# A 3x3 layer in five pairs of taps instead of six, with a second, row-shifted copy of its input

## The chip, the cores and the metric

The kernel runs on one NeuronCore of a Trainium2 chip. The metric is the device time in microseconds (us) of one launch, lower is better; the median of several runs is quoted. Engines are named as in the profile: PE (TensorE matmuls), PEld (its weight loads), DVE (VectorE), ACT (ScalarE), POOL (GpSimd), SP (SyncE, which issues all of this kernel's DMAs; SPq is its queue).

## What is computed

A batch of 16 images, 256 channels, 32 x 32 pixels, in float32, goes through two stages.

```python
# stage 0: attention block
xn   = group_norm(x, 32 groups) * gn_w + gn_b
qkv  = einsum('oc,bchw->bohw', qkv_w, xn) + qkv_b        # q, k, v: 4 heads of 64
attn = softmax(einsum('bhdm,bhdn->bhmn', q, k) / 8)      # 1024 x 1024 per head
out  = einsum('bhmn,bhdn->bhdm', attn, v)
x    = x + einsum('oc,bchw->bohw', proj_w, out) + proj_b
# stage 1: three conv layers whose weights are mixed per image from 8 experts
rw  = sigmoid(x.mean(h, w) @ router_w.T + router_b)      # 8 gates per image
out = relu(bn1(conv1x1(x,   sum_e rw[e] * w1[e])))       # 256 -> 64
out = relu(bn2(conv3x3(out, sum_e rw[e] * w2[e])))       # 64 -> 64, padding 1
out = bn3(conv1x1(out,      sum_e rw[e] * w3[e]))        # 64 -> 256
x   = relu(out + x)
```

## The kernel before

Everything of an image lies in SBUF. The attention of image i is cut into 32 steps (STEPS): two pairs of heads, two halves of the queries, eight blocks of 128 keys. For each step PE makes the scores of two heads into one of two PSUM buffers `S` (L706 and L709, four matmuls), ACT takes the exponential into `prob` (L795), POOL adds it up over the eight key blocks (L556), and PE multiplies it with V into the bank `PV` (L722); the last is done for four steps at a time, a "turn". A further pair of matmuls per step (L688, "max fill") computes scores for a later block into the bank pair `MS`, and DVE reduces these to row maxima (L922). A fill may only write a half of `MS` when DVE has reduced what was there.

All other work is cut into jobs that stand between the steps at fixed places. PE, ACT and DVE walk through the same list in the same order. The table `PLACES` gives, for each step n, the jobs that PE does behind that step's scores and fill; `HALVES` gives those behind a turn's L722 matmuls. `WORK` places their DVE part, `ACT_WORK` and `POOL_WORK` place further work of ACT and POOL, `LOADS` the loads on SP. An entry is (kind, image offset, index): offset -1 is the image whose attention ended, for which the conv layers are done, +1 is the next one, whose q, k and v are prepared.

The jobs that matter here:

- `qk` (L582, six matmuls of 512 columns in three-term float32r form): q or k of a head pair and a half. ACT copies the bank with bias to Q or K in two halves (L810), DVE makes the remainder in two halves (L959), and only then is the bank `SB` free.
- `v` (L582, six matmuls of 256 columns): one key block of v. ACT copies it out in two pieces (L816, L817).
- `row` (L631): a row of maxima; DVE copies it out (L934).
- `proj` (L626), `gna` and `gnb` (L592, L595: statistics of the group norm), `z` (L616: sums of the softmax, into one half of `MS`).
- `conv1` (L649): ACT writes the result with batch norm and relu into `hpad`, four instructions at L840. `hpad` is a padded image of 34 x 34 pixels: partitions 0 to 63 hold the 64 channels, partitions 64 to 127 the same shifted by one pixel.
- `conv2a` and `conv2` (L662), directly behind each other in turn 5: the 3x3 layer. Since the upper partitions hold the neighbour to the right, one matmul with 128 rows computes two taps of a row: (dy, 0) with (dy, 1). The taps (dy, 2) stand alone, their upper weights are zero. So TAPS = 6 pairs, each for two halves of the image (output partitions 0 to 63 and 64 to 127 of the bank): 12 matmuls per image.
- `mix`: the weights of the three layers, mixed from 8 experts. An expert is 128 x MIX numbers, MIX = 128 + TAPS * 64 + 256 = 768. ACT multiplies each with its gate (`product`, L856), POOL adds them (L513), SP loads them (L387). conv1 waits for the last addition.

All of these jobs share one bank, `SB`. Each PE job waits until the job before it has been read out (`held`). PE therefore waits wherever two jobs with a slow reader follow each other closely.

An image's iteration runs steps 0 to 31. The first and the last image have programs of their own; the last image's conv layers come at the end with nothing beside them.

Of the kernel before, what the change touches and what calls it, by code (L numbers as in the profile page):

```python
# [89 lines left out]
WORK = {1: [("qk", 0, 6)], 2: [("proj", -1, 0)], 3: [("row", 0, 1), ("stats", 1, 0), ("stats", 1, 1), ("recip", -1, 3), ("gna", 1, 0)],  # L90
        4: [("proj", -1, 1), ("gnb", 1, 0)], 7: [("qk", 0, 7)], 8: [("proj", -1, 2)], 9: [("proj", -1, 3)],
        10: [("router", -1, 0), ("gates", -1, 0), ("row", 0, 2)], 14: [("qk", 1, 0), ("qk", 1, 1)], 16: [("qk", 1, 2)],
        18: [("row", 0, 3), ("recip", 0, 0)], 22: [("recip", 0, 1), ("qk", 1, 3)], 26: [("recip", 0, 2), ("row", 1, 0)],
        27: [("conv3", -1, 0), ("conv3", -1, 1)], 29: [("qk", 1, 4)], 31: [("qk", 1, 5), ("conv3", -1, 2), ("conv3", -1, 3)]}
# [1049 lines left out]
```

## Time and profile before

| | |
|---|---|
| runs | 2052.08, 2053.33, 2059.14 us; median 2053.33 us |
| the profiled execution | 2058.66 us, of which the traced span 2056.9 us |
| PE busy | 1891.7 us, 92% of the span |
| POOL, ACT, DVE busy | 71%, 53%, 51% |

The span is the time from the first to the last traced instruction; some 1.8 us lie outside of it. An image takes 124.2 to 125.9 us from one 3x3 layer to the next. Idle times in brackets at the end of a row are those of the row's engine just before it, with what released it. fp32 matmuls leave two records for one instruction, so the 12 matmuls of L662 show as x24.

### The profile page before, as it was taken

How to read it: one execution, taken by the hardware profiler on the slowest of the kernel's cores; microseconds unless marked ns; L12 is line 12 of the kernel's file. 1: busy time of each engine (PE TensorE's matmuls, PEld its weight loads, DVE VectorE, ACT ScalarE, POOL GpSimd, SP SyncE). 2: the span in 40 equal slices, each digit the busy share in tenths (PEclk: the TensorE clock that was granted, in tenths of full speed). 3: DMA queues.
4: the chain of work that ended last, by engine and by line, in shares of the span. 5: the costliest groups of instructions: out<-in, count | busy, mean ns of one | idle time of the engine just before them, and what ended most of it. 6: DMA issues, size and time to landing. Idle time of an engine off the chain costs nothing.

```text
span 2056.9 us, 28956 instructions
## 1 busy us (share of the span) xinstructions
PE 1891.7 (92%) x8388; PEld 1073.6 (52%) x8388; DVE 1042.4 (51%) x1812; ACT 1089.9 (53%) x1498; POOL 1453.5 (71%) x829
## 2 busy tenths in 40 slices
...
GB/s 90 46 49 62 108 83 73 82 62 92 86 88 76 59 86 82 97 77 74 80 61 107 77 77 82 62 92 87 87 82 56 83 82 97 77 68 70 57 103 82
DMA packets 94113, 161.58 MB, mean 79 GB/s; under 512 B 25600, under 2 KB 26368, under 8 KB 94080
## 3 DMA queue, kind: packets, MB, share of 16 engines
...
q8 instruction: 17, 0.28, 0.1%
...
## 4 chain that ended last, share of the span: by engine, by line
PE 78%; issue 7%; DVE 6%; ACT 5%; POOL 2%; DMA 1%; DVEq 0%; ACTq 0%; SPq 0%; POOLq 0%
PE PV L722 22%; PE SB L582 13%; PE MS L688 10%; PE S L706 9%; PE S L709 8%; PE SB L626 5%; PE SB L662 4%; DVE K L959 2%; POOL psum_p L556 2%; PE SB L671 1%; PE SB L649 1%; PE MS L616 1%; DVE mx L922 1%; ACT Q L810 1%; ACT hpad L840 1%
## 5 line engine op out<-in xcount | busy, mean ns | idle before, releaser
L556 POOL TENSOR_TENSOR psum_p<-psum_p,prob 128x1024 f32<-128x1024 f32 x384 | 914.2, 2381 | 197.5 <-ACT prob L795 178.6
L922 DVE TENSOR_REDUCE mx<-MS 128x1 f32<-128x512 f32 x998 | 641.8, 685 | 597.3 <-PE MS L688 589.3
L795 ACT ACTIVATE prob<-S 128x1024 f32<-128x1024 f32 x512 | 519.5, 1023 | 301.3 <-PE S L709 297.8
L722 PE MATMUL PV<-prob,V 128*64 128x512 f32 x2048 | 475.6, 607 | 0.0
L706 PE MATMUL S<-Q,K 128*128 128x512 f32 x1024 | 445.0, 435 | 13.0 <-ACT prob L795 10.0
L709 PE MATMUL S<-Q,K 128*128 128x512 f32 x1024 | 402.1, 393 | 0.0
L688 PE MATMUL MS<-K,Q 128*128 128x512 f32 x998 | 336.8, 405 | 34.1 <-ACT zrow L828 11.9
L722 PEld LDWEIGHTS PV<-prob,V 128*64 128x64 f32 x2048 | 137.4, 138 | 259.9 <-issue 229.7
L706 PEld LDWEIGHTS S<-Q,K 128*128 128x128 f32 x1024 | 192.5, 188 | 152.4 <-issue 86.8
L688 PEld LDWEIGHTS MS<-K,Q 128*128 128x128 f32 x998 | 184.8, 187 | 123.4 <-DVE mx L922 52.2
L513 POOL TENSOR_TENSOR mix<-mix,ex 128x768 f32<-128x768 f32 x90 | 165.0, 1833 | 74.7 <-ACT ex L856 72.8
L709 PEld LDWEIGHTS S<-Q,K 128*128 128x128 f32 x1024 | 192.9, 188 | 45.2 <-issue 14.3
L556 POOL TENSOR_TENSOR psum_p<-prob 128x1024 f32<-128x1024 f32 x64 | 152.1, 2376 | 78.5 <-ACT prob L795 78.5
L518 POOL TENSOR_TENSOR o<-o,rz 128x512 f32<-128x512 f32 x63 | 80.8, 1282 | 83.4 <-DMA rz<-z_dram 83.4
L626 PE MATMUL SB<-o,wp 128*128 128x512 f32 x244 | 117.7, 604 | 22.3 <-DVE Q L959 16.5
L856 ACT ACTIVATE ex<-ex,rw 128x768 f32<-128x768 f32 x120 | 110.6, 933 | 23.9 <-DMA ex<-in_experts_dram 23.2
L582 PE MATMUL SB<-x_hi,w_hi 128*128 128x512 f32 x246 | 102.0, 414 | 22.7 <-DVE K L959 18.8
L810 ACT ACTIVATE Q<-SB,vec 64x512 fp32r<-64x512 f32 x124 | 85.0, 685 | 68.0 <-PE SB L582 66.5
L959 DVE SCALAR_TENSOR_TENSOR Q<-SB,vec,Q 64x512 fp32r<-64x512 f32 x124 | 92.9, 749 | 52.8 <-ACT Q L810 51.9
L959 DVE SCALAR_TENSOR_TENSOR K<-SB,vec,K 64x512 fp32r<-64x512 f32 x122 | 91.5, 750 | 55.0 <-ACT K L810 53.1
L810 ACT ACTIVATE K<-SB,vec 64x512 fp32r<-64x512 f32 x122 | 83.5, 684 | 67.7 <-PE SB L582 38.3
L582 PE MATMUL SB<-x_lo,w_hi 128*128 128x512 f32 x246 | 97.2, 395 | 0.0
...
## 6 DMA issues: line engine op xcount, KB each, us to landing
ex<-in_experts_dram SPq DMA_DIRECT2D x122, 384.0 KB, 3.5
...
K<-K SPq DMA_DIRECT2D x128, 128.0 KB, 2.3
Q<-Q SPq DMA_DIRECT2D x128, 128.0 KB, 2.2
...
rz<-z_dram SPq DMA_DIRECT2D x126, 128.0 KB, 2.9
V<-v_next SPq DMA_DIRECT2D x16, 512.0 KB, 2.9
```

The source lines that it names most:

```text
L513: nc.gpsimd.tensor_tensor(mix[:, :], others, ex[:, e % 2, :], ALU.add).then_inc(mix_chain, 1)
L556: nc.gpsimd.tensor_tensor(acc, first_in, prob[:, s % PBUF, :, :], ALU.add).then_inc(add_done, 1)
L582: last = nc.tensor.matmul(dst, wl(w, c), xl(m, c), start=(k == 0), stop=(k == 3 * CC - 1))
L626: last = nc.tensor.matmul(bank, wp[:, c, oc * P:oc * P + P], o[:, c, px(hf)], start=(c == 0), stop=(c == CC - 1))
L688: nc.tensor.matmul(MS[:, nh, :], Q1[:, h, q0:q0 + P], K1[:, h, px(nh)], start=True, stop=True).then_inc(max_filled, 1)
L706: nc.tensor.matmul(S[:, s % 2, a, :], K1[:, h, kt * P:kt * P + P], Q1[:, h, px(hf)], start=True, stop=False)
L709: last = nc.tensor.matmul(S[:, s % 2, a, :], K2[:, h, kt * P:kt * P + P], Q2[:, h, px(hf)], start=False, stop=True)
L722: last = nc.tensor.matmul(PV[own(a), :], V[:, b // NH, kt, a * D:a * D + D], prob[:, s % PBUF, a, :], start=(kt == 0), stop=(kt == KT - 1))
L795: nc.scalar.activation(prob[:, s % PBUF, :, :], S[:, s % 2, :, :], ACT.Exp, scale=D ** -0.5).then_inc(exp_done, 1)
L810: nc.scalar.activation(dst[own(a), 2 * p + a, px(hf)], bank[own(a), :], ACT.Identity, bias=vec[own(a), col:col + 1]).then_inc(qk_hi, 1)
L922: nc.vector.reduce_max(mx[:, b % 2, nh, m:m + 1], MS[:, nh, :], AX.X).then_inc(max_read, 1)
L959: last = nc.vector.scalar_tensor_tensor(out=dst, in0=bank[own(a), :], scalar=vec[own(a), col:col + 1], in1=hi[own(a), h, px(hf)].bitcast(F ...
```

## The change

TAPS becomes 5. Taps (0,2) and (1,2), which stood alone, form one pair: a new tile `hrow` (128 x 1156) holds the 64 channels unshifted in its lower partitions and shifted by one row in its upper ones, so that a matmul at (0, 2) computes (0,2) and (1,2) together. Tap (2,2) stays alone and is computed from `hpad`. `hrow` is filled from the lower half of `hpad` by two DMAs on SP (64 x 1156 and 64 x 1122 floats, 289 and 280.5 KB) in step 21, behind a wait for conv1's last ACT write. `conv2a` now does four pairs from `hpad`; `conv2`, behind a new wait for both DMAs, does the fifth from `hrow`. MIX becomes 704, so that each expert's load, product and addition are 8% smaller. The host packs the weights in the new order.

The tables move: on PE, `qk` 6 goes from step 1 to 0, `qk` 7 from 5 to 6, `v` 0 of the next image from 19 to 18. On DVE, these follow (`qk` 6 to step 0), the statistics are split over steps 2 and 3, the reciprocals go from 3 to 4, 18 to 16, 26 to 27, `qk` 3 from 22 to 23, `row` 0 from 26 to 27, `qk` 5 from 31 to 30. On ACT, `normal` 0 goes from 6 to 5, product 2 from 13 to 14, product 5 from 16 to 17. On POOL, `deviations` goes from 4 to 5, mix 5 from 16 to 17, mix 6 and 7 from 18 to 19, `norm` 3, 0, 1 from 7, 19, 24 to 6, 23, 29. Of the loads, V goes from 2 to 7, two of x from 21 to 20 and 25.

```diff
-TAPS = 6
+TAPS = 5
...
-          12: [("qk", 1, 0)], 15: [("qk", 1, 1)], 16: [("qk", 1, 2)], 19: [("v", 1, 0), ("row", 0, 3), ("v", 1, 1), ("v", 1, 2)],
+          12: [("qk", 1, 0)], 15: [("qk", 1, 1)], 16: [("qk", 1, 2)], 18: [("v", 1, 0)], 19: [("row", 0, 3), ("v", 1, 1), ("v", 1, 2)],
...
-LOADS = {2: [("v1", 0, 0)], 17: [("xin", 2, 0)], 21: [("xin", 2, 1), ("xin", 2, 2)], 29: [("xin", 2, 3)]}
+LOADS = {7: [("v1", 0, 0)], 17: [("xin", 2, 0)], 20: [("xin", 2, 1)], 21: [("h", -1, 0)], 25: [("xin", 2, 2)], 29: [("xin", 2, 3)]}
...
+        hrow = sb("hrow", [P, PAD])
...
+            def copy_h(i):
+
+                sp.wait_ge(read["conv1"], i + 1)
+                sp.dma_start(hrow[own(0), :], hpad[own(0), 0:PAD]).then_inc(hrow_loaded, 16)
+                sp.dma_start(hrow[own(1), 0:PAD - PW], hpad[own(0), PW:PAD]).then_inc(hrow_loaded, 16)
...
+                        if kind == "h" and not first:
+                            copy_h(i + di)
...
+            copy_h(B - 1)
             for f in range(4):
                 store(B - 1, f)
...
-                    for tap in (range(3) if kind == "conv2a" else range(3, 6)):
-                        dy, dx = tap % 3, 2 * (tap // 3)
+                    if kind == "conv2":
+                        pe.wait_ge(hrow_loaded, 32 * i + 32)
+                    for tap in (range(4) if kind == "conv2a" else (4,)):
+                        dy, dx = ((0, 0), (1, 0), (2, 0), (2, 2), (0, 2))[tap]
+                        source = hpad if kind == "conv2a" else hrow
                         for hf in range(NH):
                             at = (dy + hf * rows_hf) * PW + dx
-                            src = hpad[:, at:at + rows_hf * PW].rearrange("p (r w) -> p r w", w=PW)[:, :, 0:W]
+                            src = source[:, at:at + rows_hf * PW].rearrange("p (r w) -> p r w", w=PW)[:, :, 0:W]
...
-    low = np.concatenate([w2[0], w2[2]], axis=2)
-    high = np.concatenate([w2[1], np.zeros_like(w2[1])], axis=2)
+    low = np.concatenate([w2[0], w2[2][:, :, 2:3], w2[2][:, :, 0:1]], axis=2)
+    high = np.concatenate([w2[1], np.zeros_like(w2[1][:, :, 0:1]), w2[2][:, :, 1:2]], axis=2)
```

How this moves PE's instructions in the loop over the images, at three places. Line numbers of the changed kernel are larger by 11 to 14: L593 is L582, L642 is L631, L676 is L662, L702 is L688, L720 and L723 are L706 and L709, L936 and L973 are DVE's L922 and L959. The rows with ISA or REGISTER_ALU are waits and register arithmetic.

First, PE around step 19, before: the end of `v` 0, the row of maxima, the start of `v` 1.

```order
L688 MATMUL MS<-K1,Q1 128x512 x2
L582 MATMUL SB<-w_hi,x_hi 128x256
L582 MATMUL SB<-w_hi,x_lo 128x256
L582 MATMUL SB<-w_lo,x_hi 128x256
L582 MATMUL SB<-w_hi,x_hi 128x256
L582 MATMUL SB<-w_hi,x_lo 128x256
L582 MATMUL SB<-w_lo,x_hi 128x256
L630 REGISTER_ALU
L631 MATMUL SB<-negeye,mx1 8x128
L582 MATMUL SB<-w_hi,x_hi 128x256
```

And after:

```order
L593 MATMUL SB<-w_hi,x_lo 128x256
L593 MATMUL SB<-w_lo,x_hi 128x256
L720 MATMUL S<-Q1,K1 128x512
L723 MATMUL S<-Q2,K2 128x512
L720 MATMUL S<-Q1,K1 128x512
L723 MATMUL S<-Q2,K2 128x512
L698 ISA
L701 ISA
L702 MATMUL MS<-K1,Q1 128x512 x2
L641 REGISTER_ALU
L642 MATMUL SB<-negeye,mx1 8x128
L593 MATMUL SB<-w_hi,x_hi 128x256
```

Step 19's scores and fill now stand between `v` 0 and the row; the row and `v` 1, and `v` 1 and `v` 2, still follow each other directly.

Second, DVE at the start of the iteration, steps 0 and 1, before:

```order
L922 TENSOR_REDUCE mx<-MS 128x1
L921 ISA
L922 TENSOR_REDUCE mx<-MS 128x1
L921 REGISTER_ALU
L922 TENSOR_REDUCE mx<-MS 128x1
L957 ISA
L959 SCALAR_TENSOR_TENSOR Q<-SB,vec,Q 64x512
L957 REGISTER_ALU
L959 SCALAR_TENSOR_TENSOR Q<-SB,vec,Q 64x512
L921 ISA
```

And after:

```order
L936 TENSOR_REDUCE mx<-MS 128x1
L971 ISA
L973 SCALAR_TENSOR_TENSOR Q<-SB,vec,Q 64x512
L971 REGISTER_ALU
L973 SCALAR_TENSOR_TENSOR Q<-SB,vec,Q 64x512
L935 ISA
L936 TENSOR_REDUCE mx<-MS 128x1
L935 REGISTER_ALU
L936 TENSOR_REDUCE mx<-MS 128x1
```

The two halves of `qk` 6 moved ahead of the reductions of step 1's fill.

Third, PE at the 3x3 layer in turn 5, before:

```order
L722 MATMUL PV<-prob,V 64x512 x8
L662 MATMUL SB<-hpad,mix 64x512 x12
L609 REGISTER_ALU
L286 ISA
L616 MATMUL MS<-psum_p,ones 32x256 x4
L706 MATMUL S<-Q1,K1 128x512
```

And after:

```order
L736 MATMUL PV<-prob,V 64x512 x8
L676 MATMUL SB<-hpad,mix 64x512 x8
L669 ISA
L676 MATMUL SB<-hrow,mix 64x512 x2
L620 REGISTER_ALU
L288 ISA
L627 MATMUL MS<-psum_p,ones 32x256 x4
L720 MATMUL S<-Q1,K1 128x512
```

Two matmuls are gone, and a wait (L669) stands ahead of the last two.

## Rows read from the trace of the kernel before

**Rows 1.** The page's part 1: busy us, share of span, instructions.

```profile
PE 1891.7 (92%) x8388; PEld 1073.6 (52%) x8388; DVE 1042.4 (51%) x1812; ACT 1089.9 (53%) x1498; POOL 1453.5 (71%) x829
```

**Rows 2.** Who PE waited for in one image, 753 to 878 us: total, times, longest.

```profile
PE SB L582 <- DVE K L959: 1.3, 2, 0.9
PE SB L626 <- DVE Q L959: 1.1, 1, 1.1
```

**Rows 3.** One line's instructions, L662: first and last start, in three images.

```profile
L662 PE MATMUL SB<-hpad,mix x24: 592/592/592, 753.1 to 757.9; 128*64 128x512 f32 x24
L662 PE MATMUL SB<-hpad,mix x24: 592/592/593, 877.5 to 882.2; 128*64 128x512 f32 x24
L662 PE MATMUL SB<-hpad,mix x24: 592/592/593, 1003.3 to 1008.0; 128*64 128x512 f32 x24
```

**Rows 4.** Timeline of turn 5: start us, us, engine, line, operation.

```profile
877.46 5.32 PE L662 MATMUL SB<-hpad,mix 128*64 128x512 f32 x24
...
882.71 0.64 PE L616 MATMUL MS<-psum_p,ones 128*32 128x256 f32 x8
```

**Rows 5.** Timeline: conv1 and its write of hpad.

```profile
863.36 1.94 PE L649 MATMUL SB<-x,mix 128*64 128x512 f32 x8
...
865.34 3.15 ACT L840 ACTIVATE hpad<-SB,bn_c,bn_s 64x512 f32<-64x512 f32 x4 [1.46 <-PE SB L649]
```

**Rows 6.** The page's part 6: DMA issues, KB each, us to landing.

```profile
ex<-in_experts_dram SPq DMA_DIRECT2D x122, 384.0 KB, 3.5
...
K<-K SPq DMA_DIRECT2D x128, 128.0 KB, 2.3
...
V<-v_next SPq DMA_DIRECT2D x16, 512.0 KB, 2.9
```

**Rows 7.** Timeline of PE, steps 18 and 19.

```profile
852.06 1.09 PE L688 MATMUL MS<-K,Q 128*128 128x512 f32 x2 [0.76 <-DVE mx L922]
...
854.97 0.28 PE L582 MATMUL SB<-w_lo,x_hi 128*128 128x256 f32 x1
855.95 0.38 PE L631 MATMUL SB<-negeye,mx 128*8 128x128 f32 x2 [0.69 <-ACT v_next L817]
856.79 0.39 PE L582 MATMUL SB<-w_hi,x_hi 128*128 128x256 f32 x1 [0.46 <-DVE mrow L934]
...
858.30 0.39 PE L582 MATMUL SB<-w_hi,x_hi 128*128 128x256 f32 x1 [0.53 <-ACT v_next L817]
```

**Rows 8.** Timeline of PE and DVE, steps 0 to 2.

```profile
790.20 0.72 PE L688 MATMUL MS<-K,Q 128*128 128x512 f32 x2 [0.91 <-ACT zrow L828]
...
794.81 1.51 DVE L959 SCALAR_TENSOR_TENSOR Q<-SB,vec,Q 64x512 fp32r<-64x512 f32 x2 [1.41 <-ACT Q L810]
...
796.45 1.98 PE L626 MATMUL SB<-o,wp 128*128 128x512 f32 x4 [1.12 <-DVE Q L959]
```

**Rows 9.** Timeline of PE in step 5.

```profile
809.55 0.50 PE L582 MATMUL SB<-x_hi,w_hi 128*128 128x512 f32 x1 [0.26 <-DVE gvar_of L949]
```

**Rows 10.** Timeline of POOL, steps 17 to 19.

```profile
858.12 1.84 POOL L513 TENSOR_TENSOR mix<-mix,ex 128x768 f32<-128x768 f32 x1
860.73 1.82 POOL L513 TENSOR_TENSOR mix<-mix,ex 128x768 f32<-128x768 f32 x1 [0.77 <-ACT ex L856]
```

**Rows 11.** Busy us by stretch: PE, PEld, DVE, ACT, POOL, granted clock, DMA share, GB/s.

```profile
358.00:361.00 3.00, 2.90 (x10) 1.89 (x12) 0.00 (x0) 1.26 (x4) 1.75 (x1) 0.50 0.28 84
...
858.00:861.00 3.00, 2.70 (x16) 1.42 (x18) 0.17 (x1) 1.52 (x5) 2.23 (x3) 1.00 0.30 62
983.00:986.00 3.00, 3.00 (x12) 1.54 (x13) 0.00 (x0) 1.27 (x3) 1.56 (x2) 0.51 0.46 112
...
1607.50:1610.50 3.00, 3.00 (x10) 1.58 (x11) 0.00 (x0) 1.27 (x3) 1.54 (x2) 0.50 0.38 112
1734.00:1737.00 3.00, 3.00 (x10) 0.93 (x11) 0.00 (x0) 1.27 (x3) 1.92 (x2) 0.52 0.62 167
```

More of the change, by code:

```diff
@@ L72 @@
 TURNS = STEPS // BATCH
-PLACES = {1: [("qk", 0, 6)], 2: [("proj", -1, 0)], 3: [("row", 0, 1)], 4: [("gna", 1, 0), ("proj", -1, 1)],
-          5: [("gnb", 1, 0), ("qk", 0, 7)], 8: [("proj", -1, 2)], 9: [("proj", -1, 3)], 10: [("router", -1, 0)], 11: [("row", 0, 2)],
[1 row of a table removed]
+PLACES = {0: [("qk", 0, 6)], 2: [("proj", -1, 0)], 3: [("row", 0, 1)], 4: [("gna", 1, 0), ("proj", -1, 1)], 5: [("gnb", 1, 0)],
+          6: [("qk", 0, 7)], 8: [("proj", -1, 2)], 9: [("proj", -1, 3)], 10: [("router", -1, 0)], 11: [("row", 0, 2)],
[1 row of a table added]
           21: [("v", 1, 3)], 22: [("qk", 1, 3)], 24: [("v", 1, 4)], 25: [("v", 1, 5)], 26: [("v", 1, 6)], 27: [("row", 1, 0)],
@@ L87 @@
 FIRST_PAIRS = 8 + AHEAD
[L90 to L94, printed above, removed]
@@ L108 @@
-LOADS = {2: [("v1", 0, 0)], 17: [("xin", 2, 0)], 21: [("xin", 2, 1), ("xin", 2, 2)], 29: [("xin", 2, 3)]}
+WORK = {0: [("qk", 0, 6)], 2: [("proj", -1, 0), ("stats", 1, 0)], 3: [("row", 0, 1), ("stats", 1, 1), ("gna", 1, 0)],
+        4: [("proj", -1, 1), ("recip", -1, 3), ("gnb", 1, 0)], 7: [("qk", 0, 7)], 8: [("proj", -1, 2)], 9: [("proj", -1, 3)],
+        10: [("router", -1, 0), ("gates", -1, 0), ("row", 0, 2)], 14: [("qk", 1, 0), ("qk", 1, 1)], 16: [("recip", 0, 0), ("qk", 1, 2)],
+        18: [("row", 0, 3)], 22: [("recip", 0, 1)], 23: [("qk", 1, 3)],
+        27: [("recip", 0, 2), ("row", 1, 0), ("conv3", -1, 0), ("conv3", -1, 1)], 29: [("qk", 1, 4)], 30: [("qk", 1, 5)],
+        31: [("conv3", -1, 2), ("conv3", -1, 3)]}
```

13 lines of the change are left out of this document (7 added, 6 removed).

## The prediction

> **What bounds the kernel now.** I read the page's busy shares first. PE is busy 92% of the span, POOL 71%, ACT and DVE about half [rows 1]. So outside the start and the end PE sets the time, and another engine counts only where PE waits for it. Next I read who PE waited for in one steady image [rows 2]. Eleven kinds of wait, 0.3 to 1.3 us each, make 7.2 us of about 124; two of them stand there. Most are waits for the shared bank `SB`: a job was computed, ACT and DVE had not read it out, and the next job was already due. Third comes the length of an image. The 3x3 layer starts at 753.1, 877.5 and 1003.3 us: 124.4 us for one image, 125.8 for the next [rows 3]. The busy table with the granted clock tells them apart: at 983 to 986 us the clock is 0.51, which is 1.2 GHz instead of 2.4 [rows 11]. There are six such falls between 350 and 1740 us, four of which stand there. Each follows the same place of the image, the waits of step 19, which in a plain image end at 858.3 us [rows 7] with the clock at 1.00 behind them [rows 11]. 877.5 - 858.3 is 19.2 us ahead of the next 3x3 layer; 1003.3 - 19.2 = 984, inside the low stretch of that image. An image with such a fall takes 1.4 to 1.6 us more.
>
> **The base of the sum.** The profiled execution took 2058.66 us, the traced span is 2056.9. The median is 2053.33, so this execution was 5.3 us slower than the median. I sum against 2058.66 and take off less where the falls of the clock stay.
>
> **Part 1, the sixth pair of taps goes.** The 12 matmuls take from 877.46 to 882.71 us, when `z` starts [rows 4]: 5.25 us, 0.875 us for each tap's two halves. The two halves use different columns of the array and overlap, so the pair, not the matmul (0.59 us each in rows 3), is the unit. One pair fewer per image is 16 x 0.875 = 14.0 us, all of it on PE. Behind the layer PE goes on with `z` and scores, and no row there shows it waiting, so nothing takes the place of the time saved in steady images.
>
> **Part 2, the new wait for hrow.** No row shows such a copy. Its bounds: a 128 KB copy inside SBUF lands in 2.3 us, a 512 KB one in 2.9, a 384 KB load from memory in 3.5 [rows 6]. The copies have 289 and 280 KB. I take 2.9 us each, nearest in size and kind, and half a us for the second issue: 3.4 us; range 2.3 to 5. `hpad` is complete at 865.34 + 3.15 = 868.5 us [rows 5]. SP reaches the copy in step 21, behind loads whose conditions hold by then, so they land at about 872. The fifth pair is due at 877.46 + 4 x 0.875 = 881.0 [rows 4]: 9 us of cover, price nothing. What is queued on SP behind its wait for conv1 are `qk` 3's two copies and a reciprocal's transfers of step 22, which aren't ready before that either. At the very end the cover is only the four pairs: 3.5 us at full clock, against 3.4, so 0 to 1.5 us once. I take 0.
>
> **Part 3, smaller experts.** An addition of 1.83 us [rows 10] falls to about 704/768 of it, 1.69. That is POOL's and ACT's time; PE sees it only at conv1, which waits for the last addition. That ends at 860.73 + 1.82 = 862.55, and conv1 starts at 863.36 [rows 5, 10]. In the new table mix 6 and 7 stand behind the sums of steps 18 and 19, where before step 19's sum (2.36 to 2.4 us, like the others) came after them; so the last mix could end later. Mix 5 is done at about 854.0 (ACT's product of 852.3 and 1.69 us), then two sums to 858.8, mix 6 to 860.4, mix 7 to 862.1. PE comes to conv1 0.8 us earlier (part 4), at 862.6. So I price it at nothing, with 0 to 0.6 us an image for the range.
>
> **Part 4, the waits that the tables move.** In step 19 `v` 0, the row, `v` 1 and `v` 2 follow each other, with waits of 0.69, 0.46 and 0.53 us [rows 7]. With `v` 0 in step 18, scores and a fill (1.4 us) lie between it and the row, and ACT's copy is done. The start of the row after the start of the last `v` 0 matmul, 855.95 - 854.97 = 0.98 us, shrinks to what back-to-back matmuls take, 0.12 to 0.2: 0.8 us gone. The other two stay. `qk` 6 in step 0 instead of 1: the 1.12 us wait of `proj` goes [rows 8], but DVE now does the two halves of `qk` 6 (1.51 us) ahead of step 1's two reductions (1.3 us). `qk` 6 comes 1.65 us earlier, DVE ends it at 796.3 - 1.65 = 794.7 and the reductions at 796.0, and step 2's fill needs these. `proj`, which waits behind this fill, starts at 796.2 instead of 796.45. So a new wait eats most of the old: 0.2 us gone. `qk` 7 in step 6: its wait of 0.26 us [rows 9] goes, but step 6's fill comes sooner after step 5's reductions; 0.1 us gone. The 0.91 us for `zrow` [rows 8], 0.76 ahead of step 18's fill [rows 7] and 1.3 us for `K` in two places [rows 2] stay, since nothing moved that they hang on. The other moves change POOL, DVE and SP at places where PE doesn't wait. Together 1.1 us an image; 15 images have these places: 16.5 us. Bounds: below, 0 if each wait moves on to the next reader; above, the whole of the three waits with the restart, 0.8 + 1.1 + 0.3 = 2.2 us, 33 us.
>
> **Part 5, the clock.** The falls begin right behind step 19's waits, where PE stood 1.7 us out of some 3.5 [rows 7]; 0.7 us of that goes. The places that keep more than 1 us of waiting close together, steps 0 to 2 with 0.91 and 1.12 us [rows 8], have no fall in any image. I therefore expect the six falls to go: 6 x 1.55 = 9.3 us. The least is 0. The page "TensorE: Matmul & The Clock Gate" of the Trainium skill, in "A second HAM failure mode: psum-queue depth-cycling", tells that frequent short idles between groups of matmuls make the clock swing between its levels; the trace agrees, since no wait at these places is over 0.7 us.
>
> **The sum.** 2058.66 - 14.0 - 0 - 0 - 16.5 - 9.3 = 2018.9, say 2019 us.
>
> **The rivals.**
>
> *The falls of the clock stay.* Then their six places are set by something else than these 0.7 us: 2019 + 9.3 = 2028 us. For it speaks that only 6 of 15 equal images have one, so the waits alone don't decide. Against it, that all six stand at one place. The table in "Why this matters for your kernels" on the same page of the Trainium skill names only idle gaps longer than any wait of this image as what drops the clock mid-kernel; by it removing 0.7 us would change nothing and the time would be this rival's, while the six rows at the lower clock behind short waits speak against that rule.
>
> *The moves bring nothing.* Each wait on `SB` is handed to the next reader, as in step 2, and only the matmuls and the clock count: 2058.66 - 14.0 - 9.3 = 2035 us. For it: PE's margin over DVE's reductions is thin everywhere, fills wait 0.76 us already. Against: step 19's row waits for two ACT copies of 0.28 us, which are long done one step later.
>
> *hrow comes late, and the kernel gets slower.* The mechanism is SP's single in-order queue. If the copy stood behind a load whose condition comes late, the fifth pair waits in each image, PE's queue behind it (`z`, the scores of step 24, thus ACT's exponentials) stands too. It eats part 1 from 0.9 us of waiting on, and with parts 4 and 5 it makes the kernel slower by 0.3% only from (39.8 + 6) / 16 = 2.9 us an image on, i.e. if the copies land after 881.0 + 2.9 = 883.9, 15 us after `hpad` is there. At that price it is 2060 or more. The rows of SBUF copies (2.3 to 2.9 us) are far from it. In the milder form, that the change doesn't save its matmuls because the fifth pair waits 0.9 us, the time is 2019 + 14 = 2033.
>
> *More goes than I count.* If DVE's order at step 0 costs nothing and all three waits go, 2058.66 - 14.0 - 33 - 9.3 = 2002; half of this is 2010.
>
> **How the numbers follow.** Forecast 0.5 (2013 to 2024); falls of the clock stay in whole or part 0.2 (2024 to 2030); moves bring little, or hrow waits a little 0.17 (2030 to 2045); more goes 0.09 (2002 to 2013); slower 0.04. The range that leaves 2 in 10 out at most is 2010 to 2037. About 0.3% of the time, 6 us, is what a measurement can tell from no change. Faster by more than that 0.94, within it 0.03, slower 0.03. Nearly all cases lie on one side because PE loses 14 us of work on the path, and only an hrow 12 us late turns it.
>
> **What would show it.** Right: L662's successor shows x20 records per image and 4.4 us; an image takes 122.3 to 122.5 us; no wait of PE for hrow's DMAs; the row in step 19 has no wait in front, while a fill waits about 0.8 to 1.2 us for DVE in step 2; the clock reads 1.00 in the middle images. Wrong: an idle time of PE at the fifth pair, one at conv1 released by POOL's mix (part 3), stretches at 0.5 of the clock behind step 19, or images of 123.4 us or more.

## The result, and the profile after

| | kernel before | changed kernel |
|---|---|---|
| time, median (range) of 4 runs each, side by side | 2053.66 us (2052.08 to 2059.14) | 2021.76 us (2020.85 to 2023.01) |
| profiled execution / its span | 2058.66 / 2056.9 us | 2022.01 / 2020.2 us |
| one plain image, between starts of the 3x3 layer (mean) | 124.29 us | 122.33 us |
| one image with a fall of the clock | 125.7 to 125.9 us | none left |
| mean granted clock of TensorE, 260 to 1880 us | 0.99, six falls | 1.00, no fall |

The changed kernel takes 0.984 of the time before, interval 0.982 to 0.986. The medians lie 31.9 us apart and the two profiled executions 36.65, because the profiled execution of the kernel before was 5 us slower than its median.

The wait list of PE for one steady image of the changed kernel answers to [rows 2] (columns: engine, what it accesses, line; what it waited for; us in total, times, longest):

```profile
PE MS L702 <- DVE mx L936: 1.6, 2, 0.9
PE SB L593 <- DVE K L973: 1.3, 2, 0.9
PE MS L702 <- ACT zrow L842: 0.9, 1, 0.9
PE SB L593 <- ACT v_next L831: 0.5, 1, 0.5
PE SB L593 <- DVE mrow L948: 0.5, 1, 0.5
...
PE S L720 <- ACT prob L809: 0.4, 1, 0.4
```

Eight kinds are left of eleven, 6.0 us of 7.2. The wait for `Q` (1.1 us) has gone, and a second wait of a fill for `mx` has come. The four records of the 3x3 layer, by their source line, in two images that follow each other, answer to [rows 3]:

```profile
L676 PE MATMUL SB<-hpad,mix x16: 592/592/592, 738.7 to 741.7; 128*64 128x512 f32 x16
L676 PE MATMUL SB<-hrow,mix x4: 592/592/592, 742.1 to 742.6; 128*64 128x512 f32 x4
...
L676 PE MATMUL SB<-hpad,mix x16: 592/592/592, 861.0 to 864.0; 128*64 128x512 f32 x16
L676 PE MATMUL SB<-hrow,mix x4: 592/592/592, 864.5 to 864.9; 128*64 128x512 f32 x4
```

The reader is to see three things: 20 records instead of 24; no gap between the pairs from `hpad` and the one from `hrow` (the matmuls of both halves start together, and a new start comes every 0.43 us throughout), hence no wait for the copy; and 861.0 - 738.7 = 122.3 us for the image.

Steps 18 and 19 in the changed kernel's timeline of PE answer to [rows 7] (start, duration, engine, line, operation, tiles, idle before and its releaser):

```profile
836.40 1.09 PE L702 MATMUL MS<-K,Q 128*128 128x512 f32 x2 [0.76 <-DVE mx L936]
...
838.95 0.61 PE L702 MATMUL MS<-K,Q 128*128 128x512 f32 x2
839.50 0.39 PE L642 MATMUL SB<-negeye,mx 128*8 128x128 f32 x2
...
840.35 0.39 PE L593 MATMUL SB<-w_hi,x_hi 128*128 128x256 f32 x1 [0.46 <-DVE mrow L948]
...
841.85 0.39 PE L593 MATMUL SB<-w_hi,x_hi 128*128 128x256 f32 x1 [0.53 <-ACT v_next L831]
```

The row of maxima (L642) stands straight behind the fill; its wait of 0.69 us is gone, the other two are the same. Steps 0 to 2, first PE and then DVE, answer to [rows 8]:

```profile
774.88 0.73 PE L702 MATMUL MS<-K,Q 128*128 128x512 f32 x2 [0.91 <-ACT zrow L842]
...
780.15 1.10 PE L702 MATMUL MS<-K,Q 128*128 128x512 f32 x2 [0.86 <-DVE mx L936]
781.08 1.88 PE L637 MATMUL SB<-o,wp 128*128 128x512 f32 x4
```

```profile
777.85 1.52 DVE L973 SCALAR_TENSOR_TENSOR Q<-SB,vec,Q 64x512 fp32r<-64x512 f32 x2 [1.15 <-ACT Q L824]
779.40 2.58 DVE L936 TENSOR_REDUCE mx<-MS 128x1 f32<-128x512 f32 x4
```

`proj` (L637) no longer waits, but the fill ahead of it does, for reductions that now start behind the 1.52 us for `Q`.

The clock and the engines by stretches (start:end, length, busy time and instructions of PE, PEld, DVE, ACT, POOL, then granted clock, DMA share, GB/s), in the changed kernel over the middle and right behind step 19, answer to [rows 11]:

```profile
260.00:1880.00 1620.00, 1534.34 (x6887) 874.58 (x6885) 847.79 (x1483) 895.83 (x1246) 1188.48 (x672) 1.00 0.30 84
841.00:844.00 3.00, 2.47 (x15) 1.37 (x15) 0.53 (x1) 1.57 (x5) 3.00 (x2) 1.00 0.40 155
```

**Where the 36.65 us between the two profiled executions went.** The first start of the 3x3 layer moved from 253.0 to 249.4 us: 3.6 (1.7 of it a wait for the DMA into `Q` that the first image no longer has). The 13 images behind it took 1625.0 us (253.0 to 1878.0) and now 1590.2 (249.4 to 1839.6): 34.8, which is 13 x 1.96 = 25.5 for a plain image, and 9.3 for the six falls. The stretch from the last of these starts to the end gave back 1.7 us: 178.9 before, 180.6 after. 3.6 + 34.8 - 1.7 = 36.7.

### The profile page after: what moved, and what is told of

Its sections match the earlier page's. It is cut to its first block, busy times and chain, and to the rows that moved or that the text cites. A ratio compares the mean times of both kernels' runs of the same rounds, so it can differ in the third digit from the quotient of the medians.

```text
span 2020.2 us, 28886 instructions
## 1 busy us (share of the span) xinstructions
PE 1868.8 (93%) x8324; PEld 1063.3 (53%) x8324; DVE 1040.8 (52%) x1812; ACT 1079.9 (53%) x1498; POOL 1437.7 (71%) x829
## 4 chain that ended last, share of the span: by engine, by line
PE 75%; issue 8%; DVE 8%; ACT 5%; POOL 3%; DMA 0%; DVEq 0%; ACTq 0%; SPq 0%; POOLq 0%
PE PV L736 21%; PE SB L593 13%; PE MS L702 9%; PE S L720 9%; PE S L723 7%; PE SB L637 5%; PE SB L676 4%; DVE mx L936 3%; DVE K L973 2%; POOL psum_p L567 2%; PE SB L660 1%; PE SB L685 1%; PE MS L627 1%; ACT hpad L854 1%; ACT Q L824 1%
## 5 line engine op out<-in xcount | busy, mean ns | idle before, releaser
L936 DVE TENSOR_REDUCE mx<-MS 128x1 f32<-128x512 f32 x998 | 642.4, 686 | 544.9 <-PE MS L702 539.7
L736 PE MATMUL PV<-prob,V 128*64 128x512 f32 x2048 | 467.7, 598 | 0.0
L720 PE MATMUL S<-Q,K 128*128 128x512 f32 x1024 | 446.7, 436 | 12.8 <-ACT prob L809 9.8
L723 PE MATMUL S<-Q,K 128*128 128x512 f32 x1024 | 402.4, 393 | 0.0
L702 PE MATMUL MS<-K,Q 128*128 128x512 f32 x998 | 340.3, 409 | 48.7 <-DVE mx L936 24.8
L720 PEld LDWEIGHTS S<-Q,K 128*128 128x128 f32 x1024 | 192.6, 188 | 151.2 <-issue 98.2
L702 PEld LDWEIGHTS MS<-K,Q 128*128 128x128 f32 x998 | 185.2, 188 | 143.9 <-DVE mx L936 76.7
L723 PEld LDWEIGHTS S<-Q,K 128*128 128x128 f32 x1024 | 193.2, 189 | 43.8 <-issue 14.3
L524 POOL TENSOR_TENSOR mix<-mix,ex 128x704 f32<-128x704 f32 x90 | 152.6, 1696 | 46.1 <-ACT ex L870 43.1
L973 DVE SCALAR_TENSOR_TENSOR K<-SB,vec,K 64x512 fp32r<-64x512 f32 x122 | 91.4, 750 | 71.7 <-ACT K L824 70.3
L637 PE MATMUL SB<-o,wp 128*128 128x512 f32 x244 | 117.7, 605 | 5.8 <-DVE gsum L956 5.1
L870 ACT ACTIVATE ex<-ex,rw 128x704 f32<-128x704 f32 x120 | 102.7, 879 | 36.7 <-DMA ex<-in_experts_dram 32.7
L973 DVE SCALAR_TENSOR_TENSOR Q<-SB,vec,Q 64x512 fp32r<-64x512 f32 x124 | 92.8, 749 | 52.7 <-ACT Q L824 51.8
L593 PE MATMUL SB<-x_hi,w_hi 128*128 128x512 f32 x246 | 100.3, 408 | 18.9 <-DVE K L973 18.9
L593 PE MATMUL SB<-x_lo,w_hi 128*128 128x512 f32 x246 | 97.2, 395 | 0.0
```

Source lines behind the costliest of these rows:

```text
L524: nc.gpsimd.tensor_tensor(mix[:, :], others, ex[:, e % 2, :], ALU.add).then_inc(mix_chain, 1)
L593: last = nc.tensor.matmul(dst, wl(w, c), xl(m, c), start=(k == 0), stop=(k == 3 * CC - 1))
L637: last = nc.tensor.matmul(bank, wp[:, c, oc * P:oc * P + P], o[:, c, px(hf)], start=(c == 0), stop=(c == CC - 1))
L702: nc.tensor.matmul(MS[:, nh, :], Q1[:, h, q0:q0 + P], K1[:, h, px(nh)], start=True, stop=True).then_inc(max_filled, 1)
L720: nc.tensor.matmul(S[:, s % 2, a, :], K1[:, h, kt * P:kt * P + P], Q1[:, h, px(hf)], start=True, stop=False)
L723: last = nc.tensor.matmul(S[:, s % 2, a, :], K2[:, h, kt * P:kt * P + P], Q2[:, h, px(hf)], start=False, stop=True)
```

## Experiments

All edits are against the changed kernel unless "before" is named. Each batch was timed beside the kernel before, on another chip each time. That kernel's median was 2060.1 us beside the first four runs, 2058.8 beside the next four and 2058.3 beside the last three, against 2053.7 beside the changed kernel, which was not timed again. In ratios, the changed kernel stands at 0.984; a ratio that differs from this by 0.002 or 0.003 can come from the kernel before alone, and so can a few us between medians. What an edit does to a steady image is therefore read from the traces. "Plain image" is the mean of those without a fall; "falls" counts the images with one behind the first 3x3 layer.

| experiment | median, us | ratio to before (interval) | plain image, us | falls |
|---|---|---|---|---|
| pairs_only | 2042.76 | 0.991 (0.990 to 0.993) | 123.49 | 4 |
| moves_only | 2041.35 | 0.991 (0.989 to 0.993) | 123.60 | 0 |
| v0_only | 2038.43 | 0.990 (0.988 to 0.991) | 123.51 | 0 |
| v0_back | 2034.51 | 0.988 (0.986 to 0.989) | 123.10 | 1 |
| late_copy | 2051.68 | 0.997 (0.996 to 0.999) | 123.9 to 124.4 | 0 |
| no_copy | 2023.03 | 0.982 (0.980 to 0.983) | 122.31 | 0 |
| qk6_back | 2027.04 | 0.984 (0.983 to 0.986) | 122.49 | 0 |
| mix_back | 2020.01 | 0.981 (0.980 to 0.982) | 122.35 | 0 |
| v_spread | 2042.72 | 0.993 (0.990 to 0.995) | 123.62 | 4 |
| v_spread_qk5 | 2047.78 | 0.995 (0.993 to 0.996) | 123.80 | 5 |
| all_three | 2008.68 | 0.976 (0.973 to 0.978) | 121.56 | 0 |

### The two halves of the change apart

**pairs_only** keeps the five pairs, the copies and the smaller experts, and takes the tables of the kernel before.

PLACES, WORK, ACT_WORK and POOL_WORK are those of the kernel before word for word, and LOADS with the copy added:

```diff
-LOADS = {7: [("v1", 0, 0)], 17: [("xin", 2, 0)], 20: [("xin", 2, 1)], 21: [("h", -1, 0)], 25: [("xin", 2, 2)], 29: [("xin", 2, 3)]}
+LOADS = {2: [("v1", 0, 0)], 17: [("xin", 2, 0)], 21: [("xin", 2, 1), ("xin", 2, 2), ("h", -1, 0)], 29: [("xin", 2, 3)]}
```

> The changed kernel with all tables of places of the kernel before (the copy to hrow is added in step 21). Theory: a pair is 0.875 us of PE's path, 16 x 0.875 = 14.0 us; the waits of step 19 (0.69, 0.46, 0.53) stay, and with them the falls of the clock to 1.2 GHz behind step 19. So 2053.7 - 14 = 2040 us, an image of 123.4 us without a fall and 125.0 with one. Rival A (matmuls alone change the clock): no falls, 2058.7 - 14 - 9.3 = 2035. Rival B (the fifth pair waits for hrow or something else takes the place of the pair): 2045 to 2054.

Measured 2042.76 us (2040.22 to 2045.64). A plain image takes 123.49 us, 0.8 less than before: the price of one pair of taps. The copy and the smaller experts are in it too, but PE's eleven waits add up to 7.2 us as before. The falls did not go: four images take 125.1 us. Two of them, in stretches behind step 19:

```profile
731.00:734.00 3.00, 2.91 (x10) 1.57 (x12) 0.00 (x0) 1.25 (x4) 1.57 (x2) 0.58 0.18 65
1103.00:1106.00 3.00, 2.87 (x10) 1.56 (x12) 0.00 (x0) 1.29 (x4) 1.61 (x2) 0.59 0.26 84
```

They stand 372 us apart, three images; every third image has one. Fewer matmuls alone don't keep the clock up. The stretch behind the 14th start of the 3x3 layer, with three such layers in it, is 175.8 us long against 178.9 before.

**moves_only** is the kernel before with the tables of the changed one, and so with six pairs, 768 columns of each expert and no copy.

All five tables are replaced; of them the loads:

```diff
-LOADS = {2: [("v1", 0, 0)], 17: [("xin", 2, 0)], 21: [("xin", 2, 1), ("xin", 2, 2)], 29: [("xin", 2, 3)]}
+LOADS = {7: [("v1", 0, 0)], 17: [("xin", 2, 0)], 20: [("xin", 2, 1)], 25: [("xin", 2, 2)], 29: [("xin", 2, 3)]}
```

> The kernel before with the tables of places of the changed one (six pairs, experts of 768 columns, no hrow). Theory: waits of 1.1 us an image go in 15 images and the falls of the clock go: 2058.7 - 16.5 - 9.3 = 2033; since experts stay large and mix 6 and 7 stand later, conv1 may now wait up to 0.6 us an image for the last addition, 2033 to 2042. Rival (the moves are worth nothing, waits are handed on): 2049 to 2054.

Measured 2041.35 us (2040.32 to 2042.54), 123.6 us an image and no fall. The tables alone are worth 0.7 us an image. The changed kernel is 1.27 us shorter per image, and the pair is 0.8 to 0.86 of that. Of the remaining 0.4, 0.33 is the last line of this kernel's wait list for an image, which neither the kernel before nor the changed one has:

```profile
PE SB L649 <- POOL mix L513: 0.3, 1, 0.3
```

With experts of 768 columns and the later places, POOL's last addition ends behind the point at which conv1 is due. With 704 columns it ends just ahead of it. In the changed kernel's timeline the last addition ends at 846.76 us and conv1 starts at 846.92, a margin of 0.16 us. No run changes the size of the experts alone, so that it is the size that makes this difference is argued from the lengths of the additions (1.68 us against 1.83), not shown by itself.

```profile
845.08 1.68 POOL L524 TENSOR_TENSOR mix<-mix,ex 128x704 f32<-128x704 f32 x1
...
846.92 1.94 PE L660 MATMUL SB<-x,mix 128*64 128x512 f32 x8
```

### Which move removes the falls

**v0_only** is the kernel before with one entry moved.

```diff
-          12: [("qk", 1, 0)], 15: [("qk", 1, 1)], 16: [("qk", 1, 2)], 19: [("v", 1, 0), ("row", 0, 3), ("v", 1, 1), ("v", 1, 2)],
+          12: [("qk", 1, 0)], 15: [("qk", 1, 1)], 16: [("qk", 1, 2)], 18: [("v", 1, 0)], 19: [("row", 0, 3), ("v", 1, 1), ("v", 1, 2)],
```

> The kernel before with one place changed: v 0 of the next image in step 18 instead of 19, on PE and ACT. Theory: 0.8 us an image go in 15 images (12 us), and with 0.7 us less of waiting in step 19 the clock never falls in the middle images (9.3 us): 2058.7 - 12 - 9.3 = 2037, granted clock 1.00 in the stretches behind step 19. Rival (the falls have another cause): six or so falls stay, 2058.7 - 12 = 2047 for an execution with six, an image of 123.4 us where the clock holds and 125.0 where it falls.

Measured 2038.43 us (2037.88 to 2039.23): 123.51 us an image, 0.78 less than before, and no fall. The middle of this kernel reads

```profile
260.00:1880.00 1620.00, 1531.32 (x6882) 871.50 (x6881) 839.65 (x1470) 895.16 (x1237) 1193.62 (x668) 1.00 0.28 80
```

with the clock at 1.00. An image is as long as in pairs_only to 0.02 us, and that kernel, with the wait ahead of the row still in it, has four falls. So it isn't the length of the image that keeps the falls away here, it is the wait that went. One entry of one table gives 1.0 of the changed kernel's 1.6 per cent.

**v0_back** is the changed kernel with that entry put back, the reverse of the diff above.

> The changed kernel with v 0 put back to step 19, the rest unchanged. Theory: the wait of 0.69 us ahead of the row returns, 12 us, and the falls of the clock behind step 19 return, some 3 to 6 of them at 1.5 us: 2021.8 + 12 + 4.5 to 9.3 = 2038 to 2043. Rival (the falls don't hang on this wait): 2034, clock 1.00 throughout the middle.

Measured 2034.51 us (2033.0 to 2035.33): 123.1 us an image, so 0.77 lost, as expected. But three to six falls were expected back, and only one came, in one image of 124.7 us:

```profile
1216.00:1219.00 3.00, 2.82 (x10) 1.53 (x12) 0.00 (x0) 1.34 (x4) 2.67 (x3) 0.61 0.01 2
```

Each image of v0_back has the same 1.7 us of waits close together as each of pairs_only and of the kernel before. They have one, four and six falls. Of the kernels in which one of these waits is gone, those of v_spread and v_spread_qk5 below have falls, at a wait of 2.2 us elsewhere, and all others have none. So the waits let a fall happen, but they don't decide in which image it comes.

### What the copy costs

**late_copy** issues it one step later.

```diff
-LOADS = {7: [("v1", 0, 0)], 17: [("xin", 2, 0)], 20: [("xin", 2, 1)], 21: [("h", -1, 0)], 25: [("xin", 2, 2)], 29: [("xin", 2, 3)]}
+LOADS = {7: [("v1", 0, 0)], 17: [("xin", 2, 0)], 20: [("xin", 2, 1)], 22: [("h", -1, 0)], 25: [("xin", 2, 2)], 29: [("xin", 2, 3)]}
```

> The changed kernel with the copy to hrow in step 22 instead of 21, behind qk 3's copies and a reciprocal's transfers on SP's in-order queue (which issue last at 861.2 us in the changed kernel's trace, while the copy issues at 852.1). Theory: the cover of 9 us goes, the copy issues at about 861.3 and 861.9 and lands 3.2 and 4.0 us later, 865.9; the fifth pair is due at 864.5, so it waits 1.4 us an image, 16 x 1.4 = 22 us: 2044. Rival (such a wait costs nothing, since the scores behind it have slack): 2022 to 2026.

Measured 2051.68 us (2047.55 to 2054.89). The expectation was 2044. SP comes to the copy only at 871.31 us, when the 3x3 layer has started (871.0), and the fifth pair waits in all images but the last two. From its timeline and its wait list, which show two images that follow each other:

```profile
871.31 0.59 SPq L354 DMA_DIRECT2D hrow<-hpad  x1
...
875.98 1.08 PE L676 MATMUL SB<-hrow,mix 128*64 128x512 f32 x4 [1.36 <-DMA hrow<-hpad]
```

```profile
PE SB L676 <- DMA hrow<-hpad: 1.5, 1, 1.5
```

875.98 - 871.31 = 4.7 us passed from the first issue to the first use. The wait is 1.36 to 1.92 us in the 14 images, 1.6 on average, and the image 1.6 to 2.1 us longer, so some 0.2 us more than its wait; no other wait of PE grew. The run is 30 us longer than the changed kernel in the table, 27 by ratio. This is the rival in which `hrow` comes late, made by a single step: at 1.6 us an image it takes nearly all of the gain.

**no_copy** leaves both copies and the wait out and computes the fifth pair from `hpad`.

```diff
-LOADS = {7: [("v1", 0, 0)], 17: [("xin", 2, 0)], 20: [("xin", 2, 1)], 21: [("h", -1, 0)], 25: [("xin", 2, 2)], 29: [("xin", 2, 3)]}
+LOADS = {7: [("v1", 0, 0)], 17: [("xin", 2, 0)], 20: [("xin", 2, 1)], 25: [("xin", 2, 2)], 29: [("xin", 2, 3)]}
...
-            copy_h(B - 1)
-                    if kind == "conv2":
-                        pe.wait_ge(hrow_loaded, 32 * i + 32)
-                        source = hpad if kind == "conv2a" else hrow
+                        source = hpad
```

> The changed kernel without the two copies and without the wait: the fifth pair of taps is computed from hpad, so that the 3x3 layer's values differ from the reference. Theory: the copies and their wait are wholly hidden: 2019 to 2023, the same image of 122.3 us. Rival (0.57 MB more of DMA an image or the wait instruction costs something): 2 us or more faster.

Measured 2023.03 us (2019.21 to 2023.61), ratio 0.982 against the changed kernel's 0.984, which by itself leaves a few us open. The traces close this: the 13 images behind the first 3x3 layer take 1590.0 us here and 1590.2 in the changed kernel, and the waits of PE in one image are the same eight kinds, 6.0 us in all. In these images the copy costs nothing. In the changed kernel it is issued at 852.08 us, straight behind `hpad`:

```profile
848.90 3.15 ACT L854 ACTIVATE hpad<-SB,bn_c,bn_s 64x512 f32<-64x512 f32 x4 [1.47 <-PE SB L660]
852.08 0.53 SPq L354 DMA_DIRECT2D hrow<-hpad  x1
852.65 0.60 SPq L355 DMA_DIRECT2D hrow<-hpad  x1
```

The view of the DMA issues gives its durations (issues, KB each, median us from issue to landing):

```profile
hrow<-hpad SPq DMA_DIRECT2D x16, 289.0 KB, 3.2
...
hrow<-hpad SPq DMA_DIRECT2D x16, 280.5 KB, 4.0
```

It lands at about 856.7 us, and the fifth pair starts at 864.5: 7.8 us of cover.

### The smaller moves

**qk6_back** puts `qk` 6 back behind step 1.

```diff
-PLACES = {0: [("qk", 0, 6)], 2: [("proj", -1, 0)], 3: [("row", 0, 1)], 4: [("gna", 1, 0), ("proj", -1, 1)], 5: [("gnb", 1, 0)],
+PLACES = {1: [("qk", 0, 6)], 2: [("proj", -1, 0)], 3: [("row", 0, 1)], 4: [("gna", 1, 0), ("proj", -1, 1)], 5: [("gnb", 1, 0)],
...
-WORK = {0: [("qk", 0, 6)], 2: [("proj", -1, 0), ("stats", 1, 0)], 3: [("row", 0, 1), ("stats", 1, 1), ("gna", 1, 0)],
+WORK = {1: [("qk", 0, 6)], 2: [("proj", -1, 0), ("stats", 1, 0)], 3: [("row", 0, 1), ("stats", 1, 1), ("gna", 1, 0)],
```

> The changed kernel with qk 6 back in step 1 on all engines. Theory of the prediction: the move was worth 0.2 us an image, so 122.5 to 122.6 us an image and 2025. By the traces after: the wait of 1.12 us for Q was replaced by one of 0.86 for DVE's reductions, so 0.26 us or 3.9 in all. Rival (it was worth nothing): 2022. Rival (worth the whole 1.12): 2038.

Measured 2027.04 us (2025.78 to 2027.21), ratio 0.984, 122.49 us an image against 122.33. The wait for `Q` is back with 1.1 us, and that for `mx` stands once instead of twice:

```profile
PE SB L637 <- DVE Q L973: 1.1, 1, 1.1
```

So a wait of 1.1 us was traded for one of 0.9. Once in the run the move is worth more. In the first image PE waits 1.7 us for the DMA into `Q` in every kernel with `qk` 6 in step 1 (before, pairs_only, v0_only, qk6_back), and in none that has it in step 0. The spans of the two traces, 2025.3 and 2020.2 us, differ by 5.1: 2.7 ahead of the first 3x3 layer, 2.2 in the 13 images, 0.2 behind. That is the 5.3 us between the medians, and the ratios, which show no difference, miss it.

**mix_back** puts product 5, mix 5, and mix 6 and 7 one step earlier again.

```diff
-            14: [("product", -1, 2), ("product", -1, 3)], 15: [("product", -1, 4)], 17: [("product", -1, 5)], 18: [("product", -1, 6)],
+            14: [("product", -1, 2), ("product", -1, 3)], 15: [("product", -1, 4)], 16: [("product", -1, 5)], 18: [("product", -1, 6)],
...
-             11: [("mix", -1, 1)], 14: [("mix", -1, 2), ("mix", -1, 3)], 15: [("mix", -1, 4)], 17: [("mix", -1, 5)],
-             19: [("mix", -1, 6), ("mix", -1, 7)], 23: [("norm", 0, 0)], 29: [("norm", 0, 1)], 31: [("norm", 0, 2)]}
+             11: [("mix", -1, 1)], 14: [("mix", -1, 2), ("mix", -1, 3)], 15: [("mix", -1, 4)], 16: [("mix", -1, 5)],
+             18: [("mix", -1, 6), ("mix", -1, 7)], 23: [("norm", 0, 0)], 29: [("norm", 0, 1)], 31: [("norm", 0, 2)]}
```

> The changed kernel with mix 5, 6, 7 back in steps 16 and 18 on POOL and product 5 in 16 on ACT. Theory: conv1 doesn't wait for the last addition in either, so no change: 2020 to 2024, image 122.3. The kernel with the moves alone showed 0.3 us of waiting there with the larger experts, so the later place uses up nearly all slack. In the last image, where PE waits 5.1 us for the additions against 3.7 before the change, it may give 1 us back. Rival (POOL's order costs in the steady image): 121.9 us an image, 2016.

Measured 2020.01 us (2017.61 to 2022.35), ratio 0.981 (0.980 to 0.982). The steady image is the same, as the margin at conv1 was just enough. From the 14th start of the 3x3 layer to the 15th it takes 1.3 us less (115.7 against 117.0), for there conv1 waits for POOL 4.0 us instead of 5.1; but from there to the 16th it takes 1.5 us more, so that from the 14th start to the end 0.8 us is left (179.8 against 180.6). The other 1.6 us between the two traces lie ahead of the first 3x3 layer, where the clock stood at its lower level for 7 us instead of 10:

```profile
PE SB L660 <- POOL mix L524: 4.0, 1, 4.0
```

### Can the remaining waits be removed?

Two waits of step 19 and those for `K` were left. **v_spread** gives each `v` a step of its own.

```diff
-          12: [("qk", 1, 0)], 15: [("qk", 1, 1)], 16: [("qk", 1, 2)], 18: [("v", 1, 0)], 19: [("row", 0, 3), ("v", 1, 1), ("v", 1, 2)],
+          12: [("qk", 1, 0)], 15: [("qk", 1, 1)], 16: [("qk", 1, 2)], 17: [("v", 1, 0)], 18: [("v", 1, 1)], 19: [("row", 0, 3), ("v", 1, 2)],
```

> The changed kernel with v 0 in step 17 and v 1 in step 18, the row and v 2 in 19. Theory: what was gained by moving v 0 is had again at v 1: of the waits of 0.46 (row read by DVE) and 0.53 us (v copied by ACT), the second goes, 15 x 0.53 = 8 us with 0.1 us of restart each: 2021.8 - 8 to 9.5 = 2013, image 121.7. Rival (the wait is handed on, to the fill of step 18 that waits for DVE or to ACT's exponentials): 2020 to 2022, and the wait of 0.76 us of that fill grows.

Measured 2042.72 us (2042.44 to 2045.35): 21 us slower than the changed kernel (17 by ratio), not 9 faster. `v` 0 itself now waits, 0.94 us at 842.53, until DVE has read the bank of the `qk` before it, and so its copy by ACT comes later. The timeline of ACT, POOL and PE in this kernel has the cause, in order of time:

```profile
844.09 0.89 ACT L870 ACTIVATE ex<-ex,rw 128x704 f32<-128x704 f32 x1
845.14 1.72 POOL L524 TENSOR_TENSOR mix<-mix,ex 128x704 f32<-128x704 f32 x1 [3.24 <-ACT ex L870]
...
850.07 0.88 ACT L870 ACTIVATE ex<-ex,rw 128x704 f32<-128x704 f32 x1 [0.88 <-DMA ex<-in_experts_dram]
...
851.58 3.43 POOL L524 TENSOR_TENSOR mix<-mix,ex 128x704 f32<-128x704 f32 x2
...
855.06 1.94 PE L660 MATMUL SB<-x,mix 128*64 128x512 f32 x8 [2.20 <-POOL mix L524]
```

On ACT, product 5 of step 17 now stands behind the copy of `v` 0, which wasn't there before. POOL stands 3.24 us for it and then does mix 5, two sums (846.82 to 851.6), and mix 6 and 7. (The last product waits 0.88 us for its load, but is done at 850.95, ahead of POOL.) In the end conv1 waits 2.20 us. The falls of the clock are back too: four, with 124.6 us for such an image, so 1.0 us each. They no longer stand behind step 19 but at conv1, where the wait of 2.20 us is.

**v_spread_qk5** moves `qk` 5 from step 30 to 31 as well, on PE and DVE.

```diff
-          28: [("v", 1, 7)], 29: [("qk", 1, 4)], 30: [("qk", 1, 5)]}
+          28: [("v", 1, 7)], 29: [("qk", 1, 4)], 31: [("qk", 1, 5)]}
...
-        27: [("recip", 0, 2), ("row", 1, 0), ("conv3", -1, 0), ("conv3", -1, 1)], 29: [("qk", 1, 4)], 30: [("qk", 1, 5)],
-        31: [("conv3", -1, 2), ("conv3", -1, 3)]}
+        27: [("recip", 0, 2), ("row", 1, 0), ("conv3", -1, 0), ("conv3", -1, 1)], 29: [("qk", 1, 4)],
+        31: [("qk", 1, 5), ("conv3", -1, 2), ("conv3", -1, 3)]}
```

> The same, and qk 5 in step 31 instead of 30 on all engines. Theory: qk 5 no longer waits 0.9 us for DVE's last read of qk 4; 15 x 0.9 = 13.5 us less than v_spread: 2000, image 120.8. Rival (DVE does the read of qk 5 ahead of conv3's, so conv3's result is read later and the fill of step 28 or 0, or conv3's own wait, takes over): 2010 to 2014.

Measured 2047.78 us (2046.34 to 2048.1), 123.8 us an image; neither the 2000 of the expectation nor the 2010 to 2014 of its rival. In its wait list a wait for `K` of 0.9 us is gone against v_spread, but that of a fill for `mx` stands there twice again instead of once (1.6 us instead of 0.8): the wait was handed on. conv1 still waits 2.2 us.

**all_three** adds to this the earlier product and additions of mix_back.

> The same as v_spread_qk5, and mix 5 to 7 and product 5 back in steps 16 and 18, which was worth 1.3 us in the last image. Theory: 1.3 us less than v_spread_qk5, images unchanged. Rival (with a shorter step 17 to 19 PE comes to conv1 sooner and the later places of the mix had made it wait): up to 0.5 us an image less, 8 us.

Measured 2008.68 us (2008.27 to 2011.23), ratio 0.976 (0.973 to 0.978): faster than both kernels, and 39 us faster than v_spread_qk5, where 1.3 were expected and 8 by the rival. Its wait list for an image and its 3x3 layers:

```profile
PE MS L702 <- DVE mx L936: 1.6, 2, 0.9
PE SB L593 <- DVE Q L973: 0.9, 1, 0.9
PE MS L702 <- ACT zrow L842: 0.9, 1, 0.9
...
PE SB L593 <- DVE K L973: 0.3, 1, 0.3
```

```profile
L676 PE MATMUL SB<-hpad,mix x16: 592/592/592, 735.5 to 738.5; 128*64 128x512 f32 x16
...
L676 PE MATMUL SB<-hpad,mix x16: 592/592/592, 857.0 to 860.0; 128*64 128x512 f32 x16
```

857.0 - 735.5 = 121.5 us. The wait at conv1 is gone, which bears out the reading of v_spread. Product 5 and the additions moved back together, so which of them decides isn't shown. Against the changed kernel, the wait for `v_next` (0.5 us) is gone and that for `K` is 1.0 us shorter; a new one for `Q` takes 0.9 of it back. The same moves of `v` and `qk` 5 cost 26 us without the earlier product and additions (22 by ratio) and save 13 with them (17 by ratio). Against mix_back, which has the earlier product and additions already, they save 11.

## Why the prediction was right, point by point

**The base.** The sum was made against the profiled execution's 2058.66 us, and gave 39.8 us off it. 36.65 came between the profiled executions, 31.9 between the medians. That 2018.9 lies only 2.9 us below the measured median is in part luck: the base was 5 us above the median of its own kernel, and the saving was put 3 to 8 us too high. From the median the same sum gives 2013.5.

**Part 1, 14.0 us: right.** pairs_only shows 0.8 us an image, and 1.27 - 0.33 = 0.94 lies between moves_only and the changed kernel, once the wait for POOL is taken out. The starts of the pairs stand 0.86 us apart; the 0.875 of the prediction holds in addition what lies between the last pair and `z`. The unit was the pair, not the matmul of 0.59.

**Part 2, nothing: right, by a smaller margin, and at the end by luck.** The estimate was 3.4 us from the first issue to the landing; 4.6 were measured. Of the 9 us of cover 7.8 were left. The price of losing it is seen in late_copy, and it was underestimated: the prediction had the change come out slower from 2.9 us of waiting an image on, but at 1.6 us, which cost 1.87 us of image, 27 to 30 of its 32 us were gone. In the last image the copies land at 2003.82 + 3.98 = 2007.8 us. The four pairs ahead of the fifth take 3.4 us at full clock, so the fifth would have waited about 1 us. It didn't, because the granted clock was 0.50 there and the four pairs took 6.1:

```profile
2003.34 6.30 PE L676 MATMUL SB<-hpad,mix 128*64 128x512 f32 x16 [3.29 <-ACT hpad L854]
...
2009.46 1.04 PE L676 MATMUL SB<-hrow,mix 128*64 128x512 f32 x4
```

**Part 3, nothing: right in the sum, but it left out what the smaller experts do.** The forecast had the last addition end 0.5 us ahead of conv1; 0.16 us was left. moves_only shows that with 768 columns there is a wait of 0.3 us. So the smaller experts seem to pay for the later places of the additions, which would be worth 0.3 us an image or some 5 us; they aren't a side effect.

**Part 4, 16.5 us: right in steady images.** The sum of parts 1 and 4 was 0.875 + 1.1 = 1.975 us an image, and the image shrank by 1.96. `v` 0 was put at 0.8: 0.78 in v0_only, 0.77 in v0_back. `qk` 6 was put at 0.2: 0.16 in qk6_back's images. That the wait of 1.1 us would reappear as one of 0.86 at the fill had been read from DVE's order. `qk` 7 was not tested by itself; for it and all else 1.96 - 0.86 - 0.78 - 0.16 = 0.16 us is left.

**Part 5, 9.3 us: right in size and in place.** The six falls went, and 9.3 us went with them. The prediction's 984 for the place left out that this image is 1.55 us longer behind its fall; with it the waits end at 982.5, right ahead of the low stretch. That `v` 0 does it is shown by v0_only. That the rule behind it is only half of the matter is shown by v0_back: the same waits, one fall. The step "the falls go because 0.7 of 1.7 us go" names what lets a fall happen, not what sets it off. The page "TensorE: Matmul & The Clock Gate" of the Trainium skill names, in "Why this matters for your kernels", only longer idle gaps than any here as a cause of a drop mid-kernel; the six falls of the kernel before, four in pairs_only and one in v0_back stand behind waits of at most 0.76 us each, so the rows decide against that rule. The section "A second HAM failure mode: psum-queue depth-cycling" of the same page of the Trainium skill, on frequent short idles, agrees with them.

**What was missing: the two ends.** The sum knew 15 or 16 equal images. In the 13 in the middle it came out: 13 x 1.975 + 9.3 = 35.0 us, measured 34.8. For the two ends it had the other 4.8, and they gave 1.9. The first image gave 3.6, of which 1.7 is the wait for a DMA that had not been looked at and that goes with `qk` 6. Such a difference at the start is uncertain by some 1.5 us: the first 3x3 layer starts at 249.4 us in the changed kernel, at 247.8 in mix_back and at 251.0 in no_copy. The stretch at the end lost 1.7 us instead of gaining a share. There PE's queue is short and the additions are the bound. The changed kernel's wait list from 1843 us on has

```profile
PE SB L660 <- POOL mix L524: 5.1, 1, 5.1
...
PE MS L624 <- POOL psum_p L567: 2.6, 1, 2.6
```

where before these were 3.7 and 1.5 us. The halves of the change part here. From the 14th start of the 3x3 layer on, pairs_only is 3.1 us shorter than the kernel before, v0_only the same and moves_only 5.4 us longer (184.3 against 178.9; conv1 waits 5.7 us for POOL there and the second wait is 2.5). So the loss comes with the moved tables, and not with `v` 0; the later places of the additions, free in a steady image, are not free where nothing else is left to do. mix_back returned 0.8 us of it. The clock is lower there too, 0.83 against 0.90 over the last 63 us:

```profile
1957.00:2020.00 63.00, 43.70 (x156) 16.80 (x152) 23.81 (x45) 17.98 (x25) 19.35 (x11) 0.83 0.24 77
```

How much of the loss is the clock and how much the waits was not taken apart.

**The rivals.** "The falls stay" would have left images of 125 us; there are none. "The moves bring nothing" fell by half: the wait was handed on at `qk` 6, but not at `v` 0. "hrow late" needed one step later on SP, no more. "More goes" did not come.

## What stays open

Which image has a fall. Equal images with equal waits have it in every third (pairs_only), in six images of the run (before) or in one (v0_back). The length of the image alone isn't it, by pairs_only and v0_only. What else decides isn't shown by any run. Also what in the moved tables, beside the additions, lengthens the end, and what the lower clock has to do with it.
